# Stacked keys fetched into 64 partitions and copied to the other 64 by VectorE

## The chip, the cores and the metric

One NeuronCore of a Trainium2 chip runs the whole program. The metric is the device time of one execution in microseconds, as the median of several runs. Beside it stands one profiled execution; its span goes from its first to its last instruction.

## The reference, cut to what matters

```
x = x + xattn0(layernorm(x), ctx, mask)      # 8 elements, 112 rows, 512 features; 375 context tokens
x = x + ffn0(layernorm(x))                   # quantized, hidden width 1408
x = x + xattn1(layernorm(x), ctx, mask)      # 16 heads of 32
x = x + ffn1(layernorm(x))                   # integer weights, hidden width 1408

xattn1:  q = (x Wq + bq), k = (ctx Wk + bk), v = (ctx Wv + bv), split into heads
         scores[b, h, s, t] = clip(sum_d q[b, h, s, d] * k[b, h, t, d] / sqrt(32), -50, 50)
         probs = softmax(mask(scores));  out = (probs v) Wo + bo -> scaled -> layernorm
```

The change is in how `k` and `q` of the second attention are laid out for the scores.

## The kernel before, in words

Five queues of instructions (PE, ACT, DVE, POOL, SP) are written out by hand and meet through semaphores. Every queue runs in order, so an instruction that waits holds all behind it. SP issues the transfers.

Keys and values of the second attention are computed early, beside the first attention and the first feed-forward part. Keys are kept as two f16 numbers, a high part and the rest (`khl[g]`, 128 partitions = 4 heads x 32, g = 0 to 3 being the group of four heads). They are spilled to HBM, into `k_scratch`, by `kv_spill`, four transfers to a piece. Queries are split in the same way into `qhl`.

The score of one head is a sum over 32 features, and all four products of (high, low) keys and (high, low) queries are wanted. So a row of the 128-row contraction stands for a feature d, a key part u and a query part v. That is what the "stacks" are: `kst[b % 2]` holds each key row for both query parts, `qst` each query row for both key parts.

- Before, row 64u + 2d + v. `keys_fetch(sp, b, g)` reads each of the 64 rows (u, d) twice into 128 partitions, one transfer of 128 x 3072 bytes per element b and group g, 32 in all. `queries_stack` moves query rows inside SBUF, eight transfers of 64 partitions for each half n of the elements and pair of groups.
- `kst` has two buffers. SP fetches the keys of element b + 2 once `scores` of element b, group g, are done.

The attention stage lasts from about 250 us to 354 us. PE runs `scores` two steps (groups) ahead of `values`; a step is m = 4b + g. For each element b, the orders around the change are:

```
PE   [project(b-4), spread(b-1)]  then for g: scores(4b+g+2), [spread(b-1) after g=0 if b < 4], values(b, g)
DVE  invert(b-1), clip(4b+1), [context_low(b-3)], normalize(b-1), [delta_variance(b-4), turned_low],
     clip(4b+2), [x3_statistics(b-4)], clip(4b+3), [x3_shift], [wo low part at b=3], clip(4b+4)
POOL fold(b, 0), value_bias(b-1), fold(b, 1)           (folds for b < 4 only)
SP   keys_fetch(b+2, 0..3), [queries_stack(1, 1) at b=0], values_fetch(b+2), [integers_load]
```

`scores` (L1527) writes 448 columns for each of three chunks of keys; ACT takes the exponential (`e`, L1253); DVE clips it (`clip`, L1946) before `values` (L1544) may read it. `scores(4b)`, the first of an element, waits for `kst_loaded`; it comes at g = 2 of element b - 1. `invert` (L1952) and `spread` (L1564) make the reciprocal sums, `normalize` (L1958) applies them, `value_bias` (L637, POOL) follows `normalize`, and `fold` (L1025, L1027, POOL) adds up exponentials that PE needs at the end of `values(b, 3)` (L1556). `project` is L673, `context_low` L686, the w_o low part L2001. Before the loop stand four `query(1, g)` (L1497) between `scores(0)` and `scores(1)`, and `query_low` on DVE (L1913), behind `scales` (L1967).

Of the kernel before, what the change touches and what calls it, by code (L numbers as in the profile page):

```python
# [30 lines left out]
P = 128  # L31
# [22 lines left out]
def build(nc, x_in, ctx_tok, ctx_feat, mask_row, mask_tok, w1, w2, w3, wq, wk, wv, wo, bq, bk, bv, bo,  # L54
          gamma, beta, res_scale, wg, sg, wu, su, wd, sd, out):
    with ExitStack() as ctx:
# [76 lines left out]
        kv_raw = [at(f"kv_raw{q}", [P, KC, TP], F32, 124480 + q * 12288 + 6144) for q in range(3)]  # L133
        khl = [at(f"khl{g}", [P, 2, TP], F16, 195456 + g * 1536) for g in range(G)]
        vsp = at("vsp", [P, TC, D], F32, 201600)
        k_scratch = nc.dram_tensor("k_scratch", (B, 2, HD, G, 4, TP), F16).ap()
        v_scratch = nc.dram_tensor("v_scratch", (B, P, TC, D), F32).ap()
        ct_loaded = [sem(f"ct_loaded{q}") for q in range(3)]
        ct_hi = sem("ct_hi")
# [91 lines left out]
        def kv_spill(sp, p):  # L231

            b, (kind, n) = KV_ORDER[p // NP], piece(p)
            kv_wait_read(sp, p)
            if kind == "k":
                for hh in range(4):
                    sp.dma_start(k_scratch[b, :, :, n, hh].rearrange("u d t -> d u t"),  # L237
                                 khl[n][32 * hh:32 * hh + 32]).then_inc(k_spilled[n], 16)
            else:
                sp.dma_start(v_scratch[b, :, n], vsp[:, n]).then_inc(v_spilled[n], 16)  # L240
# [10 lines left out]
        kst = [at(f"kst{q}", [P, G, 4, TP], F16, 123136 + q * 12288) for q in range(2)]  # L251
        vst = [at(f"vst{q}", [P, TC, D], F32, 147712 + q * 6144) for q in range(2)]
        kst_loaded = [sem(f"kst_loaded{q}") for q in range(2)]
        vst_loaded = [sem(f"vst_loaded{q}") for q in range(2)]

        def keys_fetch(sp, b, g):

            sp.dma_start(kst[b % 2][:, g].rearrange("p h t -> p (h t)"),
                         k_scratch[b, :, :, g].rearrange("u d h (o t) -> (u d) o (h t)", o=1)
                         .to_broadcast([2 * HD, 2, 4 * TP])).then_inc(kst_loaded[b % 2], 16)  # L260

        def values_fetch(sp, b, q):
            sp.dma_start(vst[q][:], v_scratch[b]).then_inc(vst_loaded[q], 16)
# [290 lines left out]
        def queries_stack(sp, n, pair):  # L554

            gs_of = slice(2 * pair, 2 * pair + 2)
            sp.wait_ge(q_lo, G * n + 2 * pair + 2)
            for u in range(2):
                for hh in range(4):
                    sp.dma_start(qst[n][64 * u:64 * u + 64, hh, gs_of].rearrange("p g s -> p (g s)"),  # L560
                                 qhl[n][32 * hh:32 * hh + 32, :, gs_of].rearrange("d v g s -> d v (g s)")).then_inc(q_stacked[n][pair], 16)

        e = [at(f"e{r}", [P, TC, 4 * S], F32, 56576 + r * 5376) for r in range(4)]
        rz = at("rz", [P, S], F32, 78080)
# [776 lines left out]
        def _(pe):  # L1341
# [173 lines left out]

            def scores(m):
                b, g = m // G, m % G
                if g == 0:
                    pe.wait_ge(kst_loaded[b % 2], 16 * G * (b // 2 + 1))
                if b % 4 == 0 and g % 2 == 0:  # L1520
                    pe.wait_ge(q_stacked[b // 4][g // 2], STACK)
                if m == 0:
                    pe.wait_ge(c_lo, ALL_PARTS)
                for c in range(TC):
                    after(pe, e_raw, TC * m + c - 3)
                    for hh in range(4):
                        mm = pe.matmul(psum[:, D_S + (TC * g + c) % 4, hh * S:(hh + 1) * S], kst[b % 2][:, g, hh, c * P:(c + 1) * P],  # L1527
                                       qst[b // 4][:, hh, g, b % 4 * S:(b % 4 + 1) * S], start=True, stop=True)
                    mm.then_inc(s_sum, 1)
# [122 lines left out]
        def _(dve):  # L1652
# [318 lines left out]
            dve.sem_inc(res_ready, KC)  # L1971
            scales(0, 0, 0)
            scales(1, 1, 1)
            query_low(1, 0)
            query_low(1, 1)
            clip(0)
# [3 lines left out]
            for b in range(B):  # L1980
                if b:
                    invert(b - 1)
                if b:
                    clip(G * b + 1)
                if b >= 3:
                    context_low(dve, b - 3)
                if b:
# [3 lines left out]
                if b >= 5:  # L1991
                    turned_low(dve, b - 5)
                clip(G * b + 2)
                if b >= 4:
                    x3_statistics(dve, b - 4)
                clip(G * b + 3)
# [121 lines left out]
```

## Time and profile before

| | us |
|---|---|
| median of 3 runs | 472.92 (471.49 to 474.95) |
| the profiled execution, its time | 472.69 |
| its span | 471.0 |
| PE busy | 443.2 (94%) |
| DVE busy | 316.1 (67%) |
| ACT busy | 244.7 (52%) |
| POOL busy | 111.0 (24%) |

The 1.7 us between span and time lie outside of the instructions. The mean granted clock of PE is 0.993 of full speed. The chain that ended last is 68% PE, 12% DVE, 7% SP's queue and 4% DMA.

### The profile page before, as it was taken

How to read it: one execution, taken by the hardware profiler on the slowest of the kernel's cores; microseconds unless marked ns; L12 is line 12 of the kernel's file. 1: busy time of each engine (PE TensorE's matmuls, PEld its weight loads, DVE VectorE, ACT ScalarE, POOL GpSimd, SP SyncE). 2: the span in 40 equal slices, each digit the busy share in tenths (PEclk: the TensorE clock that was granted, in tenths of full speed). 3: DMA queues.
4: the chain of work that ended last, by engine and by line, in shares of the span. 5: the costliest groups of instructions: out<-in, count | busy, mean ns of one | idle time of the engine just before them, and what ended most of it. 6: DMA issues, size and time to landing. Idle time of an engine off the chain costs nothing.

```text
span 471.0 us, 9958 instructions
## 1 busy us (share of the span) xinstructions
PE 443.2 (94%) x3838; PEld 279.1 (59%) x3847; DVE 316.1 (67%) x573; ACT 244.7 (52%) x370; POOL 111.0 (24%) x126
## 2 busy tenths in 40 slices
PE   8999899999899899999998888899999999999997
PEld 5556565655355345454555667577775565556996
DVE  4995596679867877765755455888867985555111
ACT  4755744764666356464847668477744682221000
POOL 2220400025024000001084364644422251000000
PEclk9999999999999999999999899899999999999999
DMA  8998988934795145333497998766242370000111
GB/s 268 328 376 310 372 292 262 330 93 146 219 295 139 53 109 160 78 91 82 111 306 197 272 316 312 266 214 225 85 135 90 90 221 26 0 0 0 48 51 58
DMA packets 59183, 82.73 MB, mean 176 GB/s; under 512 B 20100, under 2 KB 43652, under 8 KB 57988
## 3 DMA queue, kind: packets, MB, share of 16 engines
q1 hardware_dynamic: 59136, 82.14, 55.2%
q8 instruction: 29, 0.48, 0.4%
q14 instruction: 16, 0.11, 0.1%
q10 hardware_dynamic: 2, 0.01, 0.0%
HBM read 58.76 MB, written 14.42 MB: 155 GB/s over the span
## 4 chain that ended last, share of the span: by engine, by line
PE 68%; DVE 12%; SPq 7%; DMA 4%; issue 4%; ACT 2%; POOL 2%; ACTq 0%; DVEq 0%; POOLq 0%
PE psum L1597 13%; PE psum L208 8%; PE psum L206 8%; PE psum L1647 8%; PE psum L1430 6%; PE psum L673 4%; PE psum L1544 3%; PE psum L1439 3%; PE psum L1497 3%; DMA kst<-k_scratch 2%; SPq L237 2%; PE psum L1373 2%; PE psum L1527 2%; PE psum L1548 2%; DMA w_stage<-in_w 2%
## 5 line engine op out<-in xcount | busy, mean ns | idle before, releaser
L208 PE MATMUL psum<-wv_p,kv_p 128*128 128x512 f16 x288 | 66.1, 379 | 0.5 <-DVE khl L228 0.5
L206 PE MATMUL psum<-kv_p,wk_p 128*128 128x376 f16 x384 | 66.0, 322 | 0.3 <-DVE khl L228 0.3
L1253 ACT ACTIVATE e<-psum,mask_bias 128x448 f32<-128x448 f32 x96 | 53.6, 635 | 20.6 <-PE psum L1527 16.1
L206 PEld LDWEIGHTS psum<-kv_p,wk_p 128*128 128x128 f16 x384 | 37.5, 98 | 24.6 <-issue 0.6
L208 PEld LDWEIGHTS psum<-wv_p,kv_p 128*128 128x128 f16 x288 | 28.0, 98 | 32.8 <-issue 1.0
L1946 DVE TENSOR_SCALAR e<-e 128x1344 f32<-128x1344 f32 x32 | 32.3, 1010 | 11.5 <-ACT e L1253 11.5
L1544 PE MATMUL psum<-e,vst 128*32 128x112 f32 x768 | 34.9, 266 | 3.9 <-issue 3.3
L1597 PE MATMUL psum<-xt,wg_b 128*128 128x448 f16 x176 | 36.9, 352 | 0.3 <-issue 0.3
L1597 PE MATMUL psum<-xt,wu_b 128*128 128x448 f16 x176 | 36.9, 352 | 0.0
L1647 PE MATMUL psum<-h_p,wd_r 128*128 x176 | 36.0, 366 | 0.0
L1647 PEld LDWEIGHTS psum<-h_p,wd_r 128*128 128x128 f32 x176 | 33.1, 188 | 2.7
L355 POOL TENSOR_SCALAR w_stage<-w_stage,w_stat 128x2816 f32<-128x2816 f32 x6 | 17.1, 2851 | 71.9 <-DVE w_stat L350 71.8
L1293 ACT ACTIVATE gated<-psum,gs 128x448 f32<-128x448 f32 x22 | 13.9, 631 | 38.7 <-PE psum L1597 33.5
L1527 PE MATMUL psum<-qst,kst 128*128 128x112 f16 x384 | 24.9, 215 | 3.6 <-issue 3.2
L2012 DVE SCALAR_TENSOR_TENSOR hf<-psum,sgu,gated 128x448 f32<-128x448 f32 x22 | 15.0, 682 | 19.5 <-ACT gated L1293 19.3
L1597 PEld LDWEIGHTS psum<-xt,wu_b 128*128 (+1 forms) x176 | 17.2, 98 | 16.1
L1597 PEld LDWEIGHTS psum<-xt,wg_b 128*128 (+1 forms) x176 | 17.1, 98 | 15.6 <-issue 0.5
L222 ACT ACTIVATE vsp<-psum 128x512 f32<-128x512 f32 x24 | 14.1, 589 | 23.4 <-PE psum L208 23.4
L1527 PEld LDWEIGHTS psum<-qst,kst 128*128 128x128 f16 x384 | 20.2, 98 | 8.9 <-issue 6.2
L218 ACT ACTIVATE khl<-psum,bqk 128x376 f16<-128x376 f32 x32 | 18.1, 568 | 13.8 <-PE psum L206 13.7
L1544 PEld LDWEIGHTS psum<-e,vst 128*32 128x32 f32 x768 | 19.9, 111 | 7.9 <-issue 4.6
L2064 DVE SCALAR_TENSOR_TENSOR res<-psum,sdn,x3t 128x448 f32 x8 | 5.5, 684 | 28.5 <-PE psum L1647 28.5
(197 smaller groups left out, 853.9 us busy)
## 6 DMA issues: line engine op xcount, KB each, us to landing
kst<-k_scratch SPq DMA_DIRECT2D x32, 384.0 KB, 6.3
kv_raw<-in_ctx_feat SPq DMA_DIRECT2D x12, 768.0 KB, 6.3
w_stage<-in_w SPq DMA_DIRECT2D x6, 1408.0 KB, 8.7
cn<-in_ctx_tok SPq DMA_DIRECT2D x8, 768.0 KB, 9.6
k_scratch<-khl SPq DMA_DIRECT2D x128, 48.0 KB, 2.0
v_scratch<-vsp SPq DMA_DIRECT2D x24, 256.0 KB, 2.8
vst<-v_scratch SPq DMA_DIRECT2D x8, 768.0 KB, 4.6
qst<-qhl SPq DMA_DIRECT2D x32, 112.0 KB, 5.2
```

What stands on the lines that cost most here:

```text
L206: mm = pe.matmul(psum[:, kv_bank(p), 0:TQ], wk_p[:, u, k, n * P:(n + 1) * P], src[:, v, k, 0:TQ], **ends)
L208: mm = pe.matmul(psum[:, kv_bank(p), :], src[:, u, k, n * P:(n + 1) * P], wv_p[:, v, k, :], **ends)
L218: act.activation(khl[n][:, 0, 0:TQ], psum[:, kv_bank(p), 0:TQ], ACT.Identity, bias=bqk[:, 1, n:n + 1]).then_inc(kv_hi, 1)
L355: pool.tensor_scalar(w_stage[:, w_half_of[half]], w_stage[:, w_half_of[half]], w_stat[:, 4 * n + 2:4 * n + 3], ROUND, ALU.mult, ALU.add).t ...
L673: mm = pe.matmul(psum[:, E_O, :], ctxt_p[t % 2][:, u, k, :], wo_p[:, v, k, :], start=(k, u, v) == (0, 0, 0), stop=(k, u, v) == (KC - 1, *P ...
L1253: act.activation(e[g][:, c, :], psum[:, D_S + (TC * g + c) % 4, 0:4 * S], ACT.Exp, bias=mask_bias[:, b, c:c + 1], scale=1.0 / (WS * QS)).t ...
L1430: mm = pe.matmul(psum[:, B_GU + 2 * ((q + c) % 2) + n, 0:hi - lo], xqt[q][:, k, :], w[:, k, lo:hi], start=k == 0, stop=k == KC - 1)
L1527: mm = pe.matmul(psum[:, D_S + (TC * g + c) % 4, hh * S:(hh + 1) * S], kst[b % 2][:, g, hh, c * P:(c + 1) * P], qst[b // 4][:, hh, g, b % ...
L1544: mm = pe.matmul(psum[32 * hh:32 * hh + 32, D_UZ[b][0], g * S:(g + 1) * S], vst[b % 2][:, c, (4 * g + hh) * HD:(4 * g + hh + 1) * HD], e[g ...
L1597: mm = pe.matmul(psum[:, F_GU + 2 * q + m, 0:HALF], w[:, k, bass.ts(j, P)], xt[:, u, k, a * HALF:(a + 1) * HALF], start=(k, u) == (0, 0), ...
L1647: mm = pe.matmul(psum[:, F_D + m, 0:HALF], wd_r[:, j, m * P:(m + 1) * P], h_p[:, a, u, j, :], start=(j, u) == (0, 0), stop=(j, u) == (JC - ...
L1946: dve.tensor_scalar(e[g][:], e[g][:], EXP_LOW, EXP_HIGH, ALU.max, ALU.min).then_inc(e_ready, 1)
```

## The change

The rows of both stacks are put in another order: row 64v + 2d + u instead of 64u + 2d + v. Then rows 64 to 127 of `kst` are the same as rows 0 to 63. For elements 0 to 5 (`DOUBLED = 6`) only rows 0 to 63 are fetched from HBM, half the bytes, and DVE copies them to rows 64 to 127, in two instructions per element (groups 0 and 1, groups 2 and 3). For elements 6 and 7 two transfers fetch the two halves. PE waits for the copies instead of the transfers. `queries_stack` keeps its count and sizes, with another source pattern.

```
-        k_scratch = nc.dram_tensor("k_scratch", (B, 2, HD, G, 4, TP), F16).ap()
+        k_scratch = nc.dram_tensor("k_scratch", (B, HD, 2, G, 4, TP), F16).ap()
...      kv_spill:
-                    sp.dma_start(k_scratch[b, :, :, n, hh].rearrange("u d t -> d u t"),
+                    sp.dma_start(k_scratch[b, :, :, n, hh],
...
+        DOUBLED = 6
+        def keys_loaded(eng, b):
+            eng.wait_ge(kst_loaded[b % 2], 16 * G * (b // 2 + 1 + max(b - DOUBLED + 2, 0) // 2))
+        def keys_double(dve, b, pair):
+            gs_of = slice(2 * pair, 2 * pair + 2)
+            keys_loaded(dve, b)
+            dve.tensor_copy(kst[b % 2][2 * HD:P, gs_of], kst[b % 2][0:2 * HD, gs_of]).then_inc(kst_doubled, 1)
...      keys_fetch:
-            sp.dma_start(kst[b % 2][:, g].rearrange("p h t -> p (h t)"),
-                         k_scratch[b, :, :, g].rearrange("u d h (o t) -> (u d) o (h t)", o=1)
-                         .to_broadcast([2 * HD, 2, 4 * TP])).then_inc(kst_loaded[b % 2], 16)
+            for o in range(1 if b < DOUBLED else 2):
+                sp.dma_start(kst[b % 2][64 * o:64 * o + 64, g].rearrange("p h t -> p (h t)"),
+                             k_scratch[b, :, :, g].rearrange("d u h t -> (d u) (h t)")).then_inc(kst_loaded[b % 2], 16)
...      queries_stack:
-            for u in range(2):
+            for v in range(2):
                 for hh in range(4):
-                    sp.dma_start(qst[n][64 * u:64 * u + 64, hh, gs_of].rearrange("p g s -> p (g s)"),
-                                 qhl[n][32 * hh:32 * hh + 32, :, gs_of].rearrange("d v g s -> d v (g s)")).then_inc(...)
+                    sp.dma_start(qst[n][64 * v:64 * v + 64, hh, gs_of].rearrange("p g s -> p (g s)"),
+                                 qhl[n][32 * hh:32 * hh + 32, v, gs_of].rearrange("d (o g) s -> d o (g s)", o=1)
+                                 .to_broadcast([HD, 2, 2 * HALF])).then_inc(...)
...      scores (PE):
-                if g == 0:
-                    pe.wait_ge(kst_loaded[b % 2], 16 * G * (b // 2 + 1))
+                if g % 2 == 0:
+                    if b < DOUBLED:
+                        pe.wait_ge(kst_doubled, 2 * b + g // 2 + 1)
+                    else:
+                        keys_loaded(pe, b)
...      DVE's order:
             scales(1, 1, 1)
+            keys_double(dve, 0, 0)
+            keys_double(dve, 0, 1)
             query_low(1, 0)
...
             for b in range(B):
                 ... invert(b - 1), clip(G * b + 1)
+                if b + 1 < DOUBLED:
+                    keys_double(dve, b + 1, 0)
                 ... context_low, normalize(b - 1), delta_variance, turned_low
                 clip(G * b + 2)
+                if b + 1 < DOUBLED:
+                    keys_double(dve, b + 1, 1)
                 ... x3_statistics, clip(G * b + 3)
```

## Rows read from the trace of the kernel before

**Rows 1.** Busy time by stretch: PE, PEld, DVE, ACT, POOL, granted clock, DMA share, GB/s.

```profile
262.00:274.00 12.00, 9.33 (x207) 8.04 (x200) 4.91 (x7) 6.79 (x14) 5.40 (x5) 0.86 1.07 264
...
322.00:334.00 12.00, 11.85 (x258) 9.21 (x252) 10.00 (x19) 8.59 (x17) 4.79 (x6) 1.00 0.60 194
...
386.00:432.00 46.00, 46.00 (x247) 24.15 (x246) 27.37 (x60) 10.21 (x17) 3.78 (x6) 1.00 0.06 19
```

**Rows 2.** Timeline of PE: start, duration, what [idle before, what ended it].

```profile
250.34 0.75 PE L1527 MATMUL psum<-qst,kst 128*128 128x112 f16 x12
...
258.78 0.78 PE L1544 MATMUL psum<-e,vst 128*32 128x112 f32 x24 [1.85 <-issue]
...
267.99 0.74 PE L1527 MATMUL psum<-qst,kst 128*128 128x112 f16 x6 [2.27 <-issue]
...
273.46 0.76 PE L1527 MATMUL psum<-qst,kst 128*128 128x112 f16 x12 [0.40 <-DMA kst<-k_scratch]
...
284.76 0.40 PE L1544 MATMUL psum<-e,vst 128*32 128x112 f32 x8
...
300.84 0.59 PE L1556 MATMUL psum<-zs,z_pick 128*32 128x112 f32 x16 [2.29 <-POOL zs L1027]
...
313.45 0.40 PE L1544 MATMUL psum<-e,vst 128*32 128x112 f32 x8
...
322.61 0.76 PE L1527 MATMUL psum<-qst,kst 128*128 128x112 f16 x12
```

**Rows 3.** Timeline of DVE in the attention stage.

```profile
249.84 0.22 DVE L1967 TENSOR_SCALAR gs<-sgu 128x1 f32<-128x1 f32 x2 [0.35 <-DVE sgu L1964]
...
266.16 1.18 DVE L1946 TENSOR_SCALAR e<-e 128x1344 f32<-128x1344 f32 x1
270.58 0.62 DVE L1958 TENSOR_TENSOR ctxt<-ctxt,psum 128x448 f32<-128x448 f32 x1 [3.23 <-PE psum L1564]
...
292.23 1.62 DVE L686 TENSOR_TENSOR ctxt_p<-ctxt,ctxt_p 128x512 f16<-128x512 f32 x1
...
306.73 0.62 DVE L1958 TENSOR_TENSOR ctxt<-ctxt,psum 128x448 f32<-128x448 f32 x1 [2.50 <-PE psum L1564]
...
312.51 0.83 DVE L1946 TENSOR_SCALAR e<-e 128x1344 f32<-128x1344 f32 x1
```

**Rows 4.** Timeline of POOL, element 3.

```profile
294.46 1.48 POOL L637 TENSOR_TENSOR ctxt<-ctxt,bqk 128x448 f32<-128x448 f32 x1 [1.16 <-DVE ctxt L1958]
295.90 1.75 POOL L1025 TENSOR_TENSOR zs<-e 128x448 f32<-128x448 f32 x1
297.73 3.06 POOL L1027 TENSOR_TENSOR zs<-zs,e 119x448 f32<-119x448 f32 x1
```

**Rows 5.** Timeline of SP's queue: issues of the keys of elements 2, 3 and 6.

```profile
260.82 2.55 SPq L258 DMA_DIRECT2D kst<-k_scratch  x4
...
270.19 2.71 SPq L258 DMA_DIRECT2D kst<-k_scratch  x4
...
304.36 5.73 SPq L258 DMA_DIRECT2D kst<-k_scratch  x4
```

**Rows 6.** Issue of each last group, elements 2 and 3: KB, us to landing.

```profile
kst<-k_scratch SPq DMA_DIRECT2D x1, 384.0 KB, 10.6
...
kst<-k_scratch SPq DMA_DIRECT2D x1, 384.0 KB, 11.1
```

**Rows 7.** DMA packets in 236 to 240 us (keys) and 262 to 264 (stacks).

```profile
DMA packets 494, 1.35 MB, mean 336 GB/s; under 512 B 56, under 2 KB 56, under 8 KB 494
...
DMA packets 287, 0.41 MB, mean 204 GB/s; under 512 B 59, under 2 KB 287, under 8 KB 287
```

**Rows 8.** Groups of instructions on DVE, shapes apart: count, busy, mean ns.

```profile
L363 DVE TENSOR_SCALAR w1q<-w1q 128x2816 bf16<-128x2816 bf16 x2 | 1.8, 894 | 0.1
```

**Rows 9.** PE's waits, 250 to 306 us: total, times, longest.

```profile
PE psum L1544 <- issue: 3.3, 2, 1.8
PE psum L1527 <- issue: 3.2, 2, 2.3
```

More of the change, by code:

```diff
@@ L253, in build @@
         kst_loaded = [sem(f"kst_loaded{q}") for q in range(2)]
+        kst_doubled = sem("kst_doubled")
+        DOUBLED = 6
[5 more added lines that the diff above has]
+            dve.tensor_copy(kst[b % 2][2 * HD:P, gs_of], kst[b % 2][0:2 * HD, gs_of]).then_inc(kst_doubled, 1)
         vst_loaded = [sem(f"vst_loaded{q}") for q in range(2)]
         def keys_fetch(sp, b, g):
-            sp.dma_start(kst[b % 2][:, g].rearrange("p h t -> p (h t)"),
-                         k_scratch[b, :, :, g].rearrange("u d h (o t) -> (u d) o (h t)", o=1)
-                         .to_broadcast([2 * HD, 2, 4 * TP])).then_inc(kst_loaded[b % 2], 16)
+            for o in range(1 if b < DOUBLED else 2):
+                sp.dma_start(kst[b % 2][64 * o:64 * o + 64, g].rearrange("p h t -> p (h t)"),
+                             k_scratch[b, :, :, g].rearrange("d u h t -> (d u) (h t)")).then_inc(kst_loaded[b % 2], 16)
         def values_fetch(sp, b, q):
@@ L557, in queries_stack @@
             sp.wait_ge(q_lo, G * n + 2 * pair + 2)
-            for u in range(2):
+            for v in range(2):
                 for hh in range(4):
-                    sp.dma_start(qst[n][64 * u:64 * u + 64, hh, gs_of].rearrange("p g s -> p (g s)"),
-                                 qhl[n][32 * hh:32 * hh + 32, :, gs_of].rearrange("d v g s -> d v (g s)")).then_inc(q_stacked[n][pair], 16)
+                    sp.dma_start(qst[n][64 * v:64 * v + 64, hh, gs_of].rearrange("p g s -> p (g s)"),
+                                 qhl[n][32 * hh:32 * hh + 32, v, gs_of].rearrange("d (o g) s -> d o (g s)", o=1)
+                                 .to_broadcast([HD, 2, 2 * HALF])).then_inc(q_stacked[n][pair], 16)
         e = [at(f"e{r}", [P, TC, 4 * S], F32, 56576 + r * 5376) for r in range(4)]
```

## The prediction

> **What bounds the kernel now.** I read the busy time by stretch first, because the change only touches the attention stage, then PE's timeline of that stage for its gaps, and last the other queues for what ends those gaps. PE is the bound almost everywhere: behind the stage it has no gap (46.00 busy of 46.00 us), and in the later elements of the stage neither (11.85 of 12) [rows 1]. So a delay that PE takes before 354 us is not given back later. The exception is the stretch of elements 0 to 3, where PE was busy for only 9.33 of 12 us at a granted clock of 0.86, with the DMA engines saturated (share 1.07) [rows 1]. The reader should look there for a possible gain. PE's gaps in it are [rows 2]: 1.85 us before `values(0,0)` at 258.78 (its value transfer was issued only at 254), 2.27 in the middle of `scores(6)` at 267.99, 0.40 for the keys of element 2 at 273.46, and 2.29 for POOL's fold at 300.84. Only one of the four names the keys, and it is worth 0.4 us.
>
> **The fetch.** Elements 0 to 5 move 192 KB per group instead of 384. Does a transfer of half the bytes end earlier? Two rows say how fast packets go [rows 7]. Keys, written to 128 partitions: 438 packets over 2 KB in 4 us of 16 engines, 146 ns each for 3072 bytes, 336 GB/s in all. Query stacks, written to 64 partitions: 228 packets over 512 B in 2 us, about 140 ns each for 1792 bytes, 204 GB/s, with the engines just as busy. So traffic to 64 partitions went at 60% of the rate. If the new fetch, also to 64 partitions, goes at 204 GB/s, the keys of an element (0.79 MB) take 3.9 us, against 4.4 (1.57 MB at about 360). If it keeps the rate of the old one they take 2.2. The ends are thus 0.4 and 2.2 us earlier per element. I take 0.4, since the stacks are the only row with the same number of partitions; the gap of 1792 to 3072 bytes is why the other end stays in the range.
>
> The Trainium skill, SBUF — State Buffer, section Door 1: The DMA port swizzle, says that partitions 0 to 63 reach no more ports than 0 to 31, and gives 196 GB/s for a 1 MiB transfer to them against 328 to all 128. The stacks' 204 GB/s fit that rule, which speaks against this change: by it the fetch would take an estimated 4.0 us for an element, by the old packets' rate 2.2.
>
> **The copy.** A copy handles 2 x 4 x 384 = 3072 f16 elements in a partition. The nearest row is a 16-bit to 16-bit instruction of DVE, 2816 elements in 894 ns [rows 8], so 0.98 us. Twelve of them add 11.7 us to an engine busy 67% of the time, which matters only where DVE's order sets the end. No row shows a copy from partitions 0-63 to 64-127. The lower bound is the 0.98. An upper one is the clip's rate, 1344 f32 elements in 0.83 us [rows 3], which makes 1.9 us. I take 1.0, because the type and the kind of operand match.
>
> **The new waits, element by element.** `scores(4b)` now waits for keys, then for a place in DVE's order, then for the copy. And DVE, waiting for keys, holds everything behind it: `normalize`, two clips, and through them POOL's `value_bias` and `fold`, ACT, and PE's `values`.
>
> - Element 0: the copies follow `scales`, whose last result is at about 249.6 to 250 [rows 3]. `scores(0)` ran at 250.34 [rows 2] and may start up to 0.6 later; behind it PE has the gap of 1.85 us before 258.78, which is set by a transfer and absorbs this. I leave 0.1. The copies of element 1 fall into DVE's idle time between clips around 258 and 260: nothing.
> - Element 1 (keys of element 2): the last group was issued at 262.8 and landed 10.6 us later, 273.4 [rows 5, 6]. DVE reaches the copy at 267.3, after clip(5) [rows 3], and now stands until about 273.0. Copy to 274.0, so `scores(8)` is 0.6 later than 273.46 [rows 2]. `normalize(0)`, at 270.58 before [rows 3], ends at 274.6, clip(6) at 275.5; POOL then needs 1.5 for the bias, and 1.1 and 1.7 undisturbed for the fold, which is 278.9. PE can use it at once and end the element at about 279.4, against 278.9. Net +0.5 (if the keys come 2.2 us earlier: -0.4, the old wait alone).
> - Element 2 (keys of element 3): last issue at 272.3, landing 283.4 [rows 5, 6], with 0.5 off 282.9. Copy to 283.9, `normalize(1)` 284.5, clip(10) 285.4. `values(2,2)` ran at 284.76 [rows 2], with the 0.5 from above at 285.3. So +0.1, and +0.6 if the landing doesn't move. I take +0.3.
> - Element 3: here the chain runs `normalize(2)`, bias, fold, PE at 300.84 [rows 2, 4]. The keys are there, but the copy stands ahead of `context_low` (292.23) and `normalize` [rows 3], so the whole chain slips by the copy: +1.0.
> - Element 4: the first copy of element 5 fits into DVE's idle 2.50 us before 306.73. The second stands ahead of clip(19), which ended at 313.34 [rows 3] while `values(4,3)` began at 313.45 [rows 2]. Slack 0.1, so +0.9 on PE, which is full from there on.
> - Elements 5 to 7: no copies. SP issues eight transfers instead of four for elements 6 and 7. Element 6's were issued from 304.36 to 310.1 [rows 5] and first read at 322.61 [rows 2]; four more at about 0.6 us leave some 8 us even if each takes a few us longer to land. Nothing.
>
> Spills and query stacks keep count and sizes; only addresses change, and SP's place for them stays. Nothing, with 0.5 us either way for their landings, as the first `scores` follow the stacks closely.
>
> Sum: 0.1 + 0.5 + 0.3 + 1.0 + 0.9 = 2.8 us on the profiled execution's own 472.69, so 475.5. The median of the runs is 472.92, 0.05% above it, so I don't correct.
>
> **Rivals.**
>
> - *A transfer of half the bytes takes half the time.* Keys of element 2 then land at about 271.2, those of element 3 at 279 (two fetches shorter). Elements 1 and 2 give -0.4 and 0. The copies in elements 3 and 4 still cost 1.9, and element 0 0.1: 472.69 + 1.6 = 474.3. For it speaks that the old packets were larger than those of the stacks; against it the stacks' rate.
> - *The other side: less traffic frees PE's instruction stream.* PE's gaps that nothing in the profile ends come to 6.5 us between 250 and 306 [rows 9], 4.6 without the one before 258.78, and the largest stood where the DMA share was 1.07 and was followed by the clock of 0.86 over 12 us (14% of 9.33, 1.3 us) [rows 1]. If these are instructions that come late behind saturated DMA engines, and the halved keys clear them, 5.9 us go: 474.3 - 5.9 = 468.4, or down to 466 if DVE's idle time hides part of the copies too. It decides only if the DMA share between 262 and 290 falls clearly below 1. Against it: the query stacks, not the keys, fill the engines at 262 to 266, where the largest gap is, and they are unchanged.
> - *Copies dearer than their row.* At 1.9 us instead of 1.0, elements 1 to 3 lose about 0.9 more each for the first copy, element 1 as much again for the second, element 4 0.9: 475.5 + 4.5 = 480. POOL's fold is part of this: it took 3.06 us instead of 1.7 beside a long DVE instruction [rows 4], so a copy beside `fold` can cost another 1 us per element in elements 1 to 3. The Trainium skill, SBUF — State Buffer, section Who interferes with whom, says that a VectorE copy in a two-port mode locks GpSimd out for the whole instruction. By it, an estimated copy's length could be added to each fold that it meets. Two gaps over 2 us that bring the clock down again (1.3 us each) belong here too.
> - *The change does not take the fetch off PE at all*, as the keys' wait was 0.4 us only. That is contained in the forecast.
>
> **How the numbers follow.** Forecast with small deviations 0.50, half the time 0.20, freed instruction stream 0.10, dearer copies 0.20. The likeliest gives 475.5, its own range 473.5 to 477.5. 1% is 4.7 us, about what a measurement tells from no change: faster means under 468.2, slower over 477.7. The forecast case gives 0.06 to slower, dearer copies 0.15, so 0.21, with 0.02 for what I don't see; faster gets most of the third case, 0.08. The range of 470 to 480.5 leaves out the far halves of the two outer cases.
>
> **What would show it.** Right: twelve copies of about 1.0 us; keys of 192 KB landing nearly as late as before (elements 2 and 3 at about 273 and 283); DVE idle before the copy at 267 to 273 and 281 to 283; PE's gaps at the first `scores` of elements 2 and 3 ended by DVE's copy; the fold of element 3 ending a microsecond later; a gap of 0.9 before `values(4,3)`; DMA rate near 200 GB/s while keys are fetched. Wrong: keys landing 2 us earlier, the gap in `scores(6)` gone, copies of 2 us or more, or a clock under 1.00 in a stretch that had 1.00 before.

## The result, and the profile after

The changed kernel takes 484.13 us, median of 4 runs (481.26 to 489.94), against 473.94 (471.49 to 478.01) for the kernel before beside it. The ratio is 1.0223 with a 95% interval of 1.0163 to 1.0284. The whole interval lies above the 1% that the prediction took as its line, so the kernel is slower; whether it is slower by 2% is not decided. A ratio is taken over the executions in the chip's faster state alone, so it need not be the quotient of the two medians. The prediction said 475.5 and 470 to 480.5.

The profiled execution took 481.77 us, its span is 480.0, 9.0 more than before, and the mean granted clock 0.989. From the page of the changed kernel: busy time, the chain that ended last by engine, and two rows of the DMA issues (KB, median us from issue to landing):

```profile
PE 444.9 (93%) x3847; PEld 279.5 (58%) x3847; DVE 332.2 (69%) x585; ACT 244.7 (51%) x370; POOL 113.7 (24%) x126
...
PE 63%; DVE 18%; SPq 8%; DMA 4%; issue 3%; ACT 2%; POOL 0%; DVEq 0%; ACTq 0%
...
kst<-k_scratch SPq DMA_DIRECT2D x40, 192.0 KB, 4.9
k_scratch<-khl SPq DMA_DIRECT2D x128, 48.0 KB, 2.3
```

PE is busy for 1.7 us more than before, with the same products: nearly all of it is in the line L206, 67.9 us instead of 66.0, and comes from a lower clock (below). So some 7 of the 9 us are idle time. DVE has 16.1 us more. The last row answers to one which read 2.0 us before: spills of the same size land later.

Where the time went is read off three places on PE. The timeline of PE in the changed kernel, as in [rows 2]:

```profile
50.88 3.92 PE L206 MATMUL psum<-kv_p,wk_p 128*128 128x376 f16 x12 [4.40 <-DVE khl L228]
...
242.64 2.43 PE L1510 MATMUL psum<-xnt_p,wq_p 128*128 128x448 f16 x12
...
258.33 0.77 PE L1543 MATMUL psum<-qst,kst 128*128 128x112 f16 x12 [0.60 <-DVE kst L265]
...
279.61 0.77 PE L1543 MATMUL psum<-qst,kst 128*128 128x112 f16 x12 [1.57 <-DVE kst L265]
...
307.74 0.40 PE L1560 MATMUL psum<-e,vst 128*32 128x112 f32 x8 [1.25 <-DVE e L1962]
...
322.74 0.40 PE L1560 MATMUL psum<-e,vst 128*32 128x112 f32 x8 [0.82 <-DVE e L1962]
...
364.12 1.67 PE L1613 MATMUL psum<-xt,wg_b 128*128 128x448 f16 x8 [0.31 <-issue]
```

| start on PE, us | before | after | later by |
|---|---|---|---|
| first query product of the second attention | 235.4 | 242.6 | 7.2 |
| `scores(0)` | 250.3 [rows 2] | 258.3 | 8.0 |
| first product behind the attention stage | 355.0 | 364.1 | 9.1 |

So in this one execution 7.2 of the 9 us were lost before the attention stage, where the prediction had costed nothing. The stage itself took 1.1 us more, less than the 2.8 forecast.

What ended PE's waits in the stage did change in the way that the prediction had in mind. Two groups from the page of the kernel before (busy, mean ns, idle time just before them, and what ended most of it):

```profile
L1544 PE MATMUL psum<-e,vst 128*32 128x112 f32 x768 | 34.9, 266 | 3.9 <-issue 3.3
...
L1527 PE MATMUL psum<-qst,kst 128*128 128x112 f16 x384 | 24.9, 215 | 3.6 <-issue 3.2
```

and the same two from the page of the changed kernel:

```profile
L1560 PE MATMUL psum<-e,vst 128*32 128x112 f32 x768 | 35.2, 267 | 9.4 <-DVE e L1962 5.8
...
L1543 PE MATMUL psum<-qst,kst 128*128 128x112 f16 x384 | 25.1, 216 | 3.4 <-DVE kst L265 2.2
```

PE now waits 5.8 us for DVE's clips (`values` reads what they write) and 2.2 us for the copies; before, the waits for clips came to 0.4 us. The copies reach PE mostly through the clips behind them.

The loss ahead of the stage begins in the queue of SP. Its timeline in the kernel before (start, duration of the merged issues, count), at the first spills of keys and the feature load behind them:

```profile
25.62 11.00 SPq L237 DMA_DIRECT2D k_scratch<-khl  x16
...
37.14 0.43 SPq L773 DMA_DIRECT2D kv_raw<-in_ctx_feat  x1
```

The same in the changed kernel:

```profile
27.14 13.21 SPq L237 DMA_DIRECT2D k_scratch<-khl  x16
...
41.02 0.43 SPq L786 DMA_DIRECT2D kv_raw<-in_ctx_feat  x1
```

Sixteen spills take 2.2 us longer to issue. This repeats in every profile with SP's loads in their old place: 9.9 to 11.0 us in the eight kernels with the old spills, 12.3 to 13.2 in the four with the new ones. The chain that ended last, in order of time, shows that this is on the path (start, us, what):

```profile
39.75 0.59 SPq L237
...
40.39 0.58 SPq L240
...
41.02 5.90 DMA kv_raw<-in_ctx_feat
...
46.94 1.49 ACT kv_p L244
...
48.46 1.06 DVE kv_p L248
...
50.13 0.61 DVE khl L228
...
50.88 3.92 PE psum L206 x12
```

Spills issue one behind the other, then comes the feature load, its split into halves, and PE, idle for 4.40 us. The windows of the changed kernel (busy by engine, granted clock, DMA share, GB/s; columns as in [rows 1]) show what follows on PE:

```profile
40.00:60.00 20.00, 15.60 (x73) 8.76 (x72) 7.72 (x15) 8.27 (x12) 2.50 (x1) 0.83 0.94 337
...
50.00:60.00 10.00, 9.12 (x38) 5.27 (x39) 5.71 (x12) 5.33 (x7) 2.50 (x1) 0.69 0.99 363
```

and of the kernel before:

```profile
40.00:60.00 20.00, 18.63 (x105) 10.99 (x104) 11.81 (x21) 11.89 (x17) 5.20 (x2) 1.00 0.96 353
```

The mean of 0.69 mixes the two levels. By windows of 2 us the granted clock was 1.00 (2.4 GHz) up to 48 us, 0.50 (1.2 GHz) from 50 to 56 and 1.00 again from 58. It fell while PE stood idle, from 46.5 to 50.9 us. The product L206 right behind the gap took 3.92 us. An earlier group of twelve of the same line, at 15.40 us, had taken 2.07. So beside the 4.4 us of idle time, the low clock took 1.9 us on this group alone.

### The profile page after: what moved, and what is told of

It is laid out like the page before. It is cut to its first block, busy times and chain, and to the rows that moved or that the text cites. A ratio compares the mean times of both kernels' runs of the same rounds, so it can differ in the third digit from the quotient of the medians.

```text
span 480.0 us, 9993 instructions
## 1 busy us (share of the span) xinstructions
PE 444.9 (93%) x3847; PEld 279.5 (58%) x3847; DVE 332.2 (69%) x585; ACT 244.7 (51%) x370; POOL 113.7 (24%) x126
## 4 chain that ended last, share of the span: by engine, by line
PE 63%; DVE 18%; SPq 8%; DMA 4%; issue 3%; ACT 2%; POOL 0%; DVEq 0%; ACTq 0%
PE psum L1613 13%; PE psum L206 8%; PE psum L208 8%; PE psum L1663 7%; PE psum L1443 6%; PE psum L686 3%; PE psum L1452 3%; PE psum L1510 3%; DVE e L1962 3%; SPq L237 3%; PE psum L1560 2%; PE psum L1386 2%; DMA kst<-k_scratch 2%; PE psum L1404 2%; SPq L812 2%
## 5 line engine op out<-in xcount | busy, mean ns | idle before, releaser
L206 PE MATMUL psum<-kv_p,wk_p 128*128 128x376 f16 x384 | 67.9, 328 | 4.7 <-DVE khl L228 4.7
L206 PEld LDWEIGHTS psum<-kv_p,wk_p 128*128 128x128 f16 x384 | 37.8, 99 | 30.4 <-DVE kv_p L248 4.9
L1962 DVE TENSOR_SCALAR e<-e 128x1344 f32<-128x1344 f32 x32 | 34.6, 1090 | 1.9 <-ACT e L1266 1.7
L1613 PEld LDWEIGHTS psum<-xt,wu_b 128*128 (+1 forms) x176 | 17.2, 98 | 16.1
L248 DVE TENSOR_TENSOR kv_p<-kv_raw,kv_p 128x1536 f16<-128x1536 f32 x11 | 19.6, 1785 | 9.8 <-ACT kv_p L244 9.8
## 6 DMA issues: line engine op xcount, KB each, us to landing
qst<-qhl SPq DMA_DIRECT2D x32, 112.0 KB, 4.2
```

Of the source, the lines that this page charges most:

```text
L206: mm = pe.matmul(psum[:, kv_bank(p), 0:TQ], wk_p[:, u, k, n * P:(n + 1) * P], src[:, v, k, 0:TQ], **ends)
L248: dve.tensor_tensor(kv_p[slot][:, 1], kv_raw[slot][:], kv_p[slot][:, 0], ALU.subtract).then_inc(ct_lo, 1)
L1613: mm = pe.matmul(psum[:, F_GU + 2 * q + m, 0:HALF], w[:, k, bass.ts(j, P)], xt[:, u, k, a * HALF:(a + 1) * HALF], start=(k, u) == (0, 0), ...
L1962: dve.tensor_scalar(e[g][:], e[g][:], EXP_LOW, EXP_HIGH, ALU.max, ALU.min).then_inc(e_ready, 1)
```

## The experiments

All ratios are against the kernel before, run on the same chip, with the 95% interval. The e, f and g kernels ran on three different chips, so a difference between two groups is a difference of two ratios, each with its own interval. "Start" and "stage" are from the single profile of each kernel: start of `scores(0)`, and the time from there to the first product behind the attention (104.7 us before).

| kernel | median us (range, runs) | ratio | start | stage |
|---|---|---|---|---|
| changed kernel | 484.13 (481.26 to 489.94, 4) | 1.0223 [1.0163, 1.0284] | 258.3 | 105.8 |
| e1b_old_spill | 479.76 (477.64 to 482.82, 6) | 1.0142 [1.0091, 1.0193] | 251.9 | 112.0 |
| e3b_padded | 479.25 (475.20 to 480.42, 6) | 1.0128 [1.0078, 1.0179] | 252.0 | 109.2 |
| e2b_new_spill | 488.08 (482.73 to 493.92, 6) | 1.0275 [1.0207, 1.0343] | 258.7 | 111.1 |
| e4b_no_copy | 488.59 (485.97 to 489.52, 6) | 1.0327 [1.0282, 1.0372] | 260.2 | 109.8 |
| f1_inplace | 479.16 (476.06 to 480.40, 6) | 1.0130 [1.0075, 1.0185] | 252.0 | 108.8 |
| f2_one_fetch | 674.20 (670.77 to 674.86, 6) | 1.4240 [1.4167, 1.4313] | 311.9 | 245.0 |
| f3_doubled8 | 482.24 (478.92 to 485.19, 6) | 1.0192 [1.0132, 1.0251] | 255.1 | 110.6 |
| f4_half_only | 476.01 (470.54 to 480.44, 12) | 1.0050 [1.0003, 1.0097] | 253.7 | 103.4 |
| g1_late_before | 470.99 (467.40 to 476.08, 12) | 0.9933 [0.9896, 0.9970] | 248.6 | 102.3 |
| g2_late_after | 480.01 (477.28 to 482.80, 6) | 1.0134 [1.0078, 1.0190] | 251.8 | 109.8 |
| g3_inplace_later | 476.80 (474.14 to 477.98, 12) | 1.0063 [1.0031, 1.0095] | 251.6 | 106.9 |
| g4_wait_only | 476.70 (471.67 to 479.43, 12) | 1.0045 [1.0005, 1.0086] | 254.6 | 104.6 |

One kernel scatters by 4 to 11 us from run to run, so the ratios over all runs carry the verdicts, and the single profiles show only how. For f1, f3 and f4 the quotients of the medians are higher than the ratios (1.0164, 1.0229 and 1.0097), so their last half per cent is not firm.

**e1b_old_spill: the changed kernel with the old layout of `k_scratch` and the old spills.**

```
-        k_scratch = nc.dram_tensor("k_scratch", (B, HD, 2, G, 4, TP), F16).ap()
+        k_scratch = nc.dram_tensor("k_scratch", (B, 2, HD, G, 4, TP), F16).ap()
-                    sp.dma_start(k_scratch[b, :, :, n, hh],
+                    sp.dma_start(k_scratch[b, :, :, n, hh].rearrange("u d t -> d u t"),
-                             k_scratch[b, :, :, g].rearrange("d u h t -> (d u) (h t)")
+                             k_scratch[b, :, :, g].rearrange("u d h t -> d u (h t)")
```

> The changed kernel with the scratch tensor and the spill of keys put back as they were; its 64-partition fetch reads the old layout with a three-dimensional source. Copies and query stacks stay as changed. Theory 1 (the spill's new pattern, merged to 64 rows x 1 x 384, costs SP 0.595 us instead of 0.427 per issue, and SP sets the pace up to about 50 us): spill issues back at about 0.43 us, PE's gap of 4.4 us at 50 us and the clock's dip behind it gone, the second query product reached 6 to 7 us earlier, ratio to the kernel before 1.002 to 1.008. Theory 2 (the copies on VectorE and their waits cost the time): ratio stays at 1.018 to 1.025. Theory 3 (what was lost before 60 us is scatter between executions): the median moves by less than 2 us against the changed kernel.

1.0142 instead of 1.0223: less than the changed kernel, but above the 1.002 to 1.008 expected if the spills were the main cause. `scores(0)` starts at 251.9 and PE's stretch of 40 to 60 us is back at its former state. In the window view of this kernel:

```profile
40.00:60.00 20.00, 18.38 (x104) 10.84 (x102) 11.30 (x21) 11.89 (x17) 5.20 (x2) 1.00 1.00 365
```

About 0.8% (3.8 us) lay in the spills, then, and 1.4% did not. The two intervals overlap, so the size of the 0.8% is uncertain by nearly as much again; e3b below gives the same, against the same four runs of the changed kernel. The line of the spills, by source, is in the kernel before (issue times min/median/max in ns, first and last start):

```profile
L237 SPq DMA_DIRECT2D k_scratch<-khl x128: 302/427/3856, 25.6 to 232.0; - x128
```

and in the changed kernel:

```profile
L237 SPq DMA_DIRECT2D k_scratch<-khl x128: 548/595/3569, 27.1 to 239.8; - x128
```

The median issue costs 168 ns more. Summed over all 128 it is 83.7 us instead of 62.2. The bytes are the same; the pattern of the transfer in the instruction list is not: the trace has the destination as 32 x 2 rows of 768 bytes before and as 64 x 1 rows now. In the new layout a step of d is two steps of u, so the two outer dimensions merge: the transfer of 32x2x384 elements becomes one of 64x1x384.

**e3b_padded: the new order of addresses, but unable to merge.** A third, unused place beside the two key parts.

```
-        k_scratch = nc.dram_tensor("k_scratch", (B, HD, 2, G, 4, TP), F16).ap()
+        k_scratch = nc.dram_tensor("k_scratch", (B, HD, 3, G, 4, TP), F16).ap()[:, :, 0:2]
-                             k_scratch[b, :, :, g].rearrange("d u h t -> (d u) (h t)")
+                             k_scratch[b, :, :, g].rearrange("d u h t -> d u (h t)")
```

> The changed kernel with its scratch tensor padded, (B, 32, 3, ...) of which two of three rows are used, so that the rows of a spill no longer lie at one stride and its pattern stays 32 x 2 x 384. Addresses are still in the new order. If the form of the pattern is the cause (theory 1a): spill issues of 0.43 us and the time of the kernel with the old spill within 2 us. If the order of addresses in HBM is the cause (theory 1b): landings of the spills and the time as in the changed kernel, ratio 1.018 to 1.025, whatever the issues take.

In the padded kernel the line of the spills reads:

```profile
L237 SPq DMA_DIRECT2D k_scratch<-khl x128: 302/428/2964, 24.4 to 233.0; - x128
```

Issue times of before, the destination again 32 x 2 rows, and with 1.0128 the time of e1b. So it is the merged form that costs the issue time, not the order of rows in HBM.

**e2b_new_spill: the kernel before with the new spills.** The fetch had to go in two transfers of 64 partitions.

```
-                    sp.dma_start(k_scratch[b, :, :, n, hh].rearrange("u d t -> d u t"),
+                    sp.dma_start(k_scratch[b, :, :, n, hh],
-            sp.dma_start(kst[b % 2][:, g].rearrange("p h t -> p (h t)"),
+            for u in range(2):
+                sp.dma_start(kst[b % 2][64 * u:64 * u + 64, g].rearrange("p h t -> p (h t)"),
...
```

> The kernel before with nothing but the scratch tensor and the spill's pattern of the change; the rows of keys and queries stay in the old order and there are no copies. A fetch of a group needs two transfers of 64 partitions here, each reading 32 rows twice. Theory 1 (issue time of the spills): spill issues of about 0.60 us, a gap of PE of several us near 50 us, attention stage itself within 2 us of the kernel before, ratio 1.012 to 1.020. Theory 2 (copies): ratio 1.000 to 1.004. Theory 3 (scatter): no gap near 50 us, ratio 1.000 to 1.004.

**e4b_no_copy: the changed kernel with two transfers for every element and no copies** (`DOUBLED = 0`, and no `keys_double` ahead of the loop).

> The changed kernel with DOUBLED = 0: both halves of the keys are fetched for all elements, in two transfers of 64 partitions, and VectorE copies nothing. The spill stays as changed. Theory 1: the loss before 60 us stays (5 to 7 us), the attention stage gets its old order of VectorE back; ratio 1.012 to 1.018, or higher if two transfers to 64 partitions each take as long as one to 128, which would put the keys of elements 2 and 3 some 3 to 4 us later. Theory 2 (copies cost the time): ratio 1.000 to 1.006.

1.0275 and 1.0327. Both are slower than expected. Both have the slow spills and both fetch the whole stack in 64 transfers of 64 partitions instead of 32 of 128, so neither isolates the spills. Their profiles show the two apart: the first query product of the second attention starts at 239.9 and 241.3 us (235.4 before), and then PE stands 3.78 and 3.74 us right ahead of `scores(0)`, which nothing in the profile ends and which the kernel before does not have. Such a fetch is dearer than the copies: e4b has no copy, and is 1% slower than the changed kernel.

**f1_inplace: the copies and their waits without the new fetch.** The kernel before, with twelve copies of rows 64 to 127 onto themselves, at the places of the change, and PE waiting for them.

```
+            dve.tensor_copy(kst[b % 2][2 * HD:P, gs_of], kst[b % 2][2 * HD:P, gs_of]).then_inc(kst_doubled, 1)
...
-                if g == 0:
-                    pe.wait_ge(kst_loaded[b % 2], 16 * G * (b // 2 + 1))
+                if g % 2 == 0:
+                    if b < DOUBLED:
+                        pe.wait_ge(kst_doubled, 2 * b + g // 2 + 1)
```

> The kernel before, with its one fetch into 128 partitions and its spill, plus the change's twelve copies at the change's places in VectorE's order and the change's waits of PE on them. Each copy reads and writes rows 64 to 127 in place, so no data change. It has the copies without the new fetch and the new spill. The kernel with the old spill but all the rest of the change measured 1.014. If the copies and their waits make that remainder (theory C): ratio 1.010 to 1.015. If fetches into 64 partitions make it, through the transfers of elements 6 and 7 and late instructions of PE (theory F): ratio 1.003 to 1.007, about the 2.8 us of the prediction.

1.0130 [1.0075, 1.0185], about 6.1 us, with spills and fetch untouched: all of what e1b had left. In its timeline of DVE, the first copy of element 2:

```profile
275.19 0.96 DVE L265 COPY kst<-kst 64x3072 f16<-64x3072 f16 x1 [6.56 <-DMA kst<-k_scratch]
```

and on its PE:

```profile
276.20 1.27 PE L1542 MATMUL psum<-qst,kst 128*128 128x112 f16 x12 [2.22 <-DVE kst L265]
```

DVE stands 6.56 us for the keys, and PE gets a gap of 2.22 where it had one of 0.40 [rows 2]. In this execution the keys also landed 1.7 us later than before, as the stage began 1.7 us later.

**g4_wait_only: f1 without the copies**, the waits and the count of the semaphore left.

```
-            dve.tensor_copy(kst[b % 2][2 * HD:P, gs_of], kst[b % 2][2 * HD:P, gs_of]).then_inc(kst_doubled, 1)
+            dve.sem_inc(kst_doubled, 1)
```

> The kernel before with the change's waits and no copy: VectorE waits for the keys at the change's places and then only counts up the semaphore that PE waits for. The prediction gave 0.1 to 0.6 us per element to such waits. If the wait is the main cost of the in-place copies (1.013): ratio 1.008 to 1.012. If the copies' time is: ratio 1.000 to 1.004, and the twelve copies, 0.95 us alone and up to 1.8 beside POOL, make the other 4 to 5 us.

1.0045, about 2 us, with an interval that starts at 1.0005. DVE waits as long, now with `normalize` behind the wait:

```profile
277.49 0.62 DVE L1973 TENSOR_TENSOR ctxt<-ctxt,psum 128x448 f32<-128x448 f32 x1 [6.45 <-DMA kst<-k_scratch]
```

In this one profile the stage lost nothing (104.6) and the start was 4.3 us late, ahead of all edits. Where the 2 us of the ratio lie is thus not shown by it; the difference to f1, 0.85% or 4 us with an uncertainty of some 3, is the copies.

**g3_inplace_later: f1 with the first copy of each element behind `normalize(b-1)`** instead of ahead of it.

```
-                if b + 1 < DOUBLED:
-                    keys_double(dve, b + 1, 0)
                 if b >= 3:
                     context_low(dve, b - 3)
...
+                if b + 1 < DOUBLED:
+                    keys_double(dve, b + 1, 0)
```

> The kernel before with the in-place copies (1.013), the first copy of each element now behind normalize instead of ahead of context_low and normalize. If holding normalize, and through it POOL's bias and fold, is the main part: ratio falls to 1.005 to 1.009. If the copies' own time on VectorE ahead of the clips is: the ratio stays within 0.2% of 1.013, since both clips still stand behind the same copies.

1.0063. The place of one copy, with its wait, in DVE's order is worth 0.7% (3 us, and the intervals of f1 and g3 overlap). It is not the wait alone: with the wait in its early place and no copy (g4) the cost was 0.45%. In its timeline of DVE:

```profile
270.44 0.62 DVE L1973 TENSOR_TENSOR ctxt<-ctxt,psum 128x448 f32<-128x448 f32 x1 [2.26 <-PE psum L1579]
...
274.24 0.96 DVE L265 COPY kst<-kst 64x3072 f16<-64x3072 f16 x1 [3.17 <-DMA kst<-k_scratch]
```

`normalize` runs as early as before (270.58 in [rows 3]), and only the copy and the clip behind it wait. In f1, where the copy is ahead of it, `normalize` could not run until 276.

**f3_doubled8: e1b with copies for elements 6 and 7 as well** (`DOUBLED = 8`), on PE's full chain.

> The kernel with the old spill (ratio 1.014) with DOUBLED = 8, so that elements 6 and 7 are also fetched once into 64 partitions and copied. Theory C: two more copies per element on a full chain, 0.9 us each for elements 6 and 7, so 1 to 2 us slower than with DOUBLED = 6. Theory F: the gaps of 1.7 to 3 us that PE showed near 315 and 335 us, while two times 768 KB went into 64 partitions each, are gone or shorter, which gives back 2 to 4 us: ratio 1.008 to 1.013.

1.0192 against 1.0142. The intervals overlap. If the 0.5% (2.4 us) are real, each of the four added copies costs 0.6 us on a chain that is full, less than its length; the double fetches of these elements went in exchange. This profile also had a late start, 255.1, and a granted clock of 0.83 from 50 to 60 us, with the old spills: a loss of that kind comes without the slow spills too.

**f4_half_only: half the fetch without copies.** e1b without copies, so against the kernel before it also has the new query stacks. Elements 0 and 1 are fetched in both halves, elements 2 to 7 only into the lower 64 partitions, so their upper rows are stale.

```
-            for o in range(1 if b < DOUBLED else 2):
+            for o in range(2 if b < 2 else 1):
...
```

> The kernel with the old spill, no copies, and half the keys left out: elements 0 and 1 are fetched in both halves, elements 2 to 7 only into partitions 0 to 63, and the scores of these elements use stale rows in the other half. It shows what the halved fetch alone is worth. If the fetch into 64 partitions takes as long as the whole one into 128: keys of elements 2 and 3 land within 1 us of the kernel before, ratio 0.998 to 1.004. If half the bytes take half the time: landings 2 to 4 us earlier and PE's unexplained gaps shorter, ratio 0.988 to 0.996. The double fetch of elements 0 and 1 ends before the first scores either way.

1.0050 [1.0003, 1.0097]: half the bytes, with no copy and no wait for one, make the whole no faster. A small gain can hide in it. The two-part fetch of elements 0 and 1 adds eight transfers, and in the profile PE stands 1.99 us ahead of `scores(0)`, as in e2b and e4b, and starts 3.3 us late; the stage behind it is 1.3 us shorter than before (103.4).

**f2_one_fetch: the changed kernel without copies, with one transfer to 128 partitions.** The doubling is the outermost dimension of the source, with stride 0.

```
+            src = k_scratch[b, :, :, g].rearrange("d u h t -> (d u) (h t)")
+            src = bass.AP(tensor=src.tensor, offset=src.offset, ap=[[0, 2], *src.ap])
+            sp.dma_start(kst[b % 2][:, g].rearrange("p h t -> p (h t)"), src).then_inc(kst_loaded[b % 2], 16)
```

> The changed kernel's order of rows, spill and query stacks, but no copies, and each group fetched for all elements by one transfer that reads the 64 rows twice into 128 partitions. It has the new spill without copies and without fetches into 64 partitions. Theory 1 (issue time of the spills alone): the loss before 60 us, 4 to 7 us, and nothing in the attention stage; ratio 1.009 to 1.014. The kernel with two fetches of 64 partitions and no copies measured 1.033, so if this one comes at or under 1.014, the difference of 2% is what two half transfers cost against one whole.

1.42. The view of the DMA queues for 250 to 300 us of this kernel: the busy tenths of the engines in 40 slices, and the packets.

```profile
DMA  1111111111111111111111111111111111466758
...
DMA packets 1469, 3.43 MB, mean 69 GB/s; under 512 B 137, under 2 KB 652, under 8 KB 1469
```

and the waits of PE (total, times, longest):

```profile
PE psum L1543 <- DMA kst<-k_scratch: 139.2, 6, 26.6
```

For most of this stretch the engines' mean share is a tenth and the rate some 50 GB/s. Two busy engines of sixteen would give a share of 0.125. The Trainium skill, DMA: Bandwidth & Descriptors, under How many engines (k), says that a transfer uses the largest number of engines up to 16 that divides the slowest dimension that isn't 1 of both its patterns. Here these are 2 and 128, and the trace agrees. In the kernel before they were 64 and 128, and its fetch kept all engines full (336 GB/s, [rows 7]). PE also stood 56.2 us ahead of the first `scores`, a gap that nothing in the profile ends.

**g1_late_before and g2_late_after: room in SP's queue.** If the early stage is bound by SP's issues, taking others out of it must help. Eight small loads of constants that are needed only later move from ahead of the loop over elements to the end of its round b = 3, in the kernel before (g1) and in the changed one (g2).

```
-            sp.dma_start(attend[:], mask_tok).then_inc(consts_loaded, 16)
...
+                if b == 3:
+                    sp.dma_start(attend[:], mask_tok).then_inc(consts_loaded, 16)
...
```

> The kernel before with SP's eight loads of constants (masks for tokens, scales, bias rows), which its queue issued from 12.8 to 25.6 us ahead of the first spills, moved behind element 3 of the first attention. If SP's issue time sets the pace up to 50 us: the first spill is issued near 14 us or when its piece is ready, the load of features at 37 us comes some 5 us or more earlier, PE's gap at 49 us goes; ratio 0.990 to 0.997 (0.8 to 1.4 us of gap before 50 us and what piles up behind it). If SP's queue does not matter there: 0.998 to 1.003.

> The changed kernel with the same move of the eight loads. Its spills still take 0.595 us to issue. If they cost time only because SP's queue is the bound before 50 us (theory 1), room in that queue pays for them: the gap of 4.4 us at 50 us is gone, ratio to the kernel before 1.008 to 1.014, as with the old spill or a little under. If the new spill's transfers slow something themselves, the loss stays: 1.018 or more.

SP's timeline in g1:

```profile
15.41 15.45 SPq L237 DMA_DIRECT2D k_scratch<-khl  x16
...
31.37 0.43 SPq L773 DMA_DIRECT2D kv_raw<-in_ctx_feat  x1
```

and in g2:

```profile
15.34 16.20 SPq L237 DMA_DIRECT2D k_scratch<-khl  x16
...
32.21 0.43 SPq L786 DMA_DIRECT2D kv_raw<-in_ctx_feat  x1
```

The sixteen spills start 10 to 12 us earlier, the feature load is issued at 31.4 and 32.2 us instead of 37.1 and 41.0, and PE has no idle time from 40 to 60 us in either. So SP's queue does bound the early stage: g1 is 0.67% faster than the kernel before, and the fastest of all. g2 brings the changed kernel from 1.0223 to 1.0134, which was expected if the slow spills cost time only through the queue. But it does not single them out, because the room is worth nearly as much, 0.67%, to the kernel with the fast spills. With room in both queues the two kernels are still 2.0% apart (1.0134 to 0.9933), with none 2.2%. A kernel with the old spills, the copies and the room was not run, so what the slow spills cost when there is room stays open.

## Why the prediction was wrong

**"Spills and query stacks keep count and sizes; only addresses change ... Nothing."** This step failed (it left 0.5 us either way), and it is one of the two parts of the miss. Count and size of a transfer do not give its issue time: that went from 427 to 595 ns for 128 spills, 168 ns each or 21.5 us of SP's queue in all, of which only the early ones were seen to be on the path. Shown: the form of the pattern makes the issue slow (e3b), and the old form gives back about 4 us (e1b 0.8%, e3b 0.95%, each with an uncertainty of 0.8%). In the profile the feature load was issued 3.9 us later. Of these 1.5 were there before the first changed instruction (25.62 to 27.14), and belong to the scatter between executions, and about 2.2 are spills. The idle PE, and 6 to 7 us at the low clock, add to them. The 7.2 us of this profile are thus more than the 4 us of the ratios. Other profiles say the same. The first query product started at 239.9 to 241.3 us in the three further kernels with new spills and loads in the old place. It started at 235.9 to 236.6 in five of the seven with old spills in that queue, but at 239.4 and 239.7 in the other two (f3, g4), by scatter. The sum began at the attention stage; [rows 1 to 9] hold no row of SP ahead of 250 us. A row of the spills and a look at the queue that carries them was missing.

**The copies and the waits: 2.8 us were forecast, 6.1 measured (f1).** This is the other part. The mechanism was right, the term mis-sized. The waits alone make about 2 us (g4), the copies the other 4. Two things were too small:

- *The price of a copy.* Twelve took 15.0 us, 1.26 on average, not the 0.98 from [rows 8]. The groups of instructions of the changed kernel with shapes apart, and then DVE's timeline:

```profile
L265 DVE COPY kst<-kst 64x3072 f16<-64x3072 f16 x12 | 15.0, 1260 | 4.6 <-DMA kst<-k_scratch 4.3
```

```profile
265.65 1.76 DVE L265 COPY kst<-kst 64x3072 f16<-64x3072 f16 x1
...
278.60 0.95 DVE L265 COPY kst<-kst 64x3072 f16<-64x3072 f16 x1 [3.67 <-DMA kst<-k_scratch]
...
281.01 1.57 DVE L265 COPY kst<-kst 64x3072 f16<-64x3072 f16 x1
...
300.57 1.78 DVE L265 COPY kst<-kst 64x3072 f16<-64x3072 f16 x1
...
306.01 1.67 DVE L1962 TENSOR_SCALAR e<-e 128x1344 f32<-128x1344 f32 x1
```

  and the timeline of POOL beside it:

```profile
265.45 1.14 POOL L1038 TENSOR_TENSOR zs<-e 128x448 f32<-128x448 f32 x1
...
280.29 1.48 POOL L650 TENSOR_TENSOR ctxt<-ctxt,bqk 128x448 f32<-128x448 f32 x1 [4.37 <-DVE ctxt L1974]
281.73 1.84 POOL L1038 TENSOR_TENSOR zs<-e 128x448 f32<-128x448 f32 x1
...
299.90 1.64 POOL L1040 TENSOR_TENSOR zs<-zs,e 119x448 f32<-119x448 f32 x1
```

  With POOL idle a copy takes 0.95 us, as forecast. The copies at 265.65, 281.01 and 300.57 began while POOL was in an instruction, which ended at 266.59, 281.77 and 301.54. They ended 0.81 to 0.82 us behind it, and POOL's instruction took no longer than usual (the fold at 265.45 took 1.14). Three more of the twelve did the same, so six copies took 1.14 to 1.78. The other way round, the fold at 281.73 began while DVE was in the copy, and took 1.84 instead of 1.14. This is the rival of dearer copies, by its second mechanism, and in both directions. The Trainium skill, SBUF — State Buffer, section Who interferes with whom, says that a VectorE copy in a two-port mode and a GpSimd instruction share a pair of ports, that the one that issues first holds it for its whole length, and that the other is blocked. The rows agree: the second is late by about what was left of the first.
- *The place of the copy.* The prediction named what stands behind the copy, but gave it 0.5 us at element 1. Moving the copy behind `normalize` is worth about 3 us over all elements (f1 to g3).

In the profile of the changed kernel the stage shows only +1.1 us, in those of f1, e3b and g2, which start it at 252, 4.1 to 5.1, in e1b 7.3. The difference from e1b is largely in PE's gaps that nothing in the profile ends: by the view of PE's waits over the stage they sum to 5.9 us in the changed kernel, 11.8 in e1b, 11.5 in g2, 9.0 in e3b, and 7.6 in the kernel before. The waits for the clips are alike, 5.8 and 5.5. What these gaps are stays open, and so does whether the late start has to do with it: f3 started late too (255.1), and its stage took 110.6. The parts add, 0.8% from e1b and 1.3% from f1 make 2.1, measured 2.2, within intervals of half a per cent each.

**The fetch: right in kind, somewhat too dear in size.** In the changed kernel, where only keys were fetched (243 to 249 us), the view of the DMA queues reads:

```profile
DMA packets 550, 1.37 MB, mean 228 GB/s; under 512 B 104, under 2 KB 104, under 8 KB 550
...
q1 hardware_dynamic: 550, 1.37, 102.8%
```

228 GB/s with all engines full, against 336 to 128 partitions [rows 7]: half the bytes at two thirds of the rate. By these two rates an element takes an estimated 3.5 us instead of 4.7, 1.2 earlier; the prediction's 0.4 came from 204 GB/s for the new fetch and about 360 for the old one, where its row says 336. In e1b the keys of elements 2 and 3 were issued when before's were and landed at 271.8 and 282.9 us, 1.6 and 0.6 earlier, so both between the ends of 0.4 and 2.2. It changed nothing in the time (f1 and e1b, with the old and the new fetch: 1.0130 and 1.0142), nor did f4. The rival of half the time had element 3 at 279, and falls. So does that of the freed instruction stream: from 262 to 274 us the DMA share of e1b was 1.08, before's 1.07 [rows 1], and the gaps that nothing ends grew, in f4 too (10.7 us in the stage, 7.6 before).

**Element by element.** Right in kind: the gaps at the first `scores` ended by the copy (0.60 at element 0, 1.57 at element 2), 0.82 us ahead of `values(4,3)` for 0.9 forecast, DVE idle 3.67 us for the keys of element 2. Wrong: element 3, where the fold was to end a microsecond later; PE waited there for a clip that ran beside the fold (1.25 us), not for the fold, which had been 2.29 [rows 2]. And "elements 6 and 7: nothing" is not safe. PE in e1b has two gaps that nothing in the profile ends, while SP fetches the whole keys of these elements in eight transfers:

```profile
315.37 0.29 PE L1564 MATMUL psum<-e,z_pick 128*32 128x112 f32 x3 [3.06 <-issue]
...
335.15 0.40 PE L1564 MATMUL psum<-e,z_pick 128*32 128x112 f32 x8 [1.98 <-issue]
```

The changed kernel does not show them. But f3, without the double fetch, has 1.96 and 0.45 us at these places, and f1, with the old fetch, 1.69 and 0.19, so the double fetch is not what makes them. Open.

**The range.** It took the dearer copies to 480.5 and would have held 1.3%; it had no room for a second cause of 0.8% in another stage.

## What to carry to other kernels

A new layout of a scratch tensor also changes the transfers that write it: compare the patterns of the instructions before and after, not only bytes and counts, and look at the queue that issues them where many stand in a row ahead of a load that is waited for (16 here). A copy with a wait, added to an engine's order, is priced by what stands behind it: put it as late as its reader allows. A fix that frees a queue is also to be tried on the kernel before: here it was worth nearly as much there. Half the bytes are little gain where the transfer also goes to half the partitions, and a copy on VectorE is costed with GpSimd's work beside it, not alone.

## What the runs showed of the hardware that was not expected

- SP takes longer to issue a merged pattern: 595 ns for 64x1x384, 427 ns for 32x2x384, with the same bytes to the same kind of place (128 issues each, and 428 ns again in e3b). The unchanged transfer right behind the sixteen, L240, took 0.58 us instead of 0.42, so the delay is not only in the decoding of the merged pattern. Whether it is the count of outer rows or the spreading over the engines behind it was not tried.
- A source whose outermost dimension is a repetition of 2 went at some 50 GB/s instead of 336, with a mean share of the DMA engines of a tenth.
- A VectorE copy of 3072 f16 elements in 64 partitions, to other partitions or in place: 0.95 us alone. When GpSimd was already in an instruction, it ended 0.81 to 0.82 us behind that instruction, after 1.14 to 1.78 us.
- The granted clock fell to 0.50 in an idle stretch of PE of 4.4 us and was back at 1.00 by 58 us; twelve matmuls took 3.92 us there and 2.07 at full clock.
